# A post-norm attention and int8 layer on one core: inverse softmax divisors spread by small matmuls, y scaled on VectorE

## The reference

```python
def attention(X, Wq, Wk, Wv, Wo):            # X: (4, 1024, 512), 16 query heads, 8 key heads of 64
    q, k, v = heads(X @ Wq), heads(X @ Wk), heads(X @ Wv)
    q, k = rope(q), rope(k)                  # q*cos + rotate_half(q)*sin
    att = 50 * tanh((q @ k.T) * 256**-0.5 / 50)
    att = softmax(where(causal, att, -inf))
    return concat_heads(att @ v) @ Wo
def ffn(x):                                  # int8 per token
    scale = max(absmax(x), 1e-7) / 127
    q = clip(round(x / scale), -128, 127)
    return float16((q @ weight.T) * scale * w_scale + bias)
x = layernorm(X + attention(X, ...))
out = layernorm(x + ffn(x))
```

## Time and profile before

| | us |
|---|---|
| median of 3 runs | 1561.52 (1559.03 to 1564.63) |
| the profiled execution | 1562.01, its span 1560.3 |
| PE busy in the span | 1317.1 (84%) |
| DVE busy | 1055.1 (68%) |
| ACT busy | 843.2 (54%) |
| POOL busy | 378.6 (24%) |

### The profile page before, as it was taken

How to read it: one execution, slowest core, us unless ns; L and a number is a source line. 1 busy time by engine, 2 the same in 40 slices (tenths; PEclk the granted TensorE clock), 3 DMA queues, 4 the chain that set the end, 5 groups by cost and what they waited for, 6 DMA issues and landing times.

```text
span 1560.3 us, 17566 instructions
## 1 busy us (share of the span) xinstructions
PE 1317.1 (84%) x5776; PEld 965.0 (62%) x5776; DVE 1055.1 (68%) x1334; ACT 843.2 (54%) x952; POOL 378.6 (24%) x477
## 2 busy tenths in 40 slices
PE   6489998988687999797777999979867799999564
PEld 5366776666465777575545677756655577776442
DVE  4377887763467888683456888877346788887354
ACT  4166676652227876673223877766222577788122
POOL 2231111112542111111344111111144311121354
PEclk9789999999898999899978999999999899999797
DMA  7755445366514344447621543546562344433531
GB/s 269 255 199 139 112 128 164 79 206 188 169 54 103 104 125 112 135 95 274 176 97 54 129 109 100 130 114 190 181 198 71 97 104 107 121 87 119 183 115 48
DMA packets 124715, 212.24 MB, mean 136 GB/s; under 512 B 28112, under 2 KB 70096, under 8 KB 120400
## 3 DMA queue, kind: packets, MB, share of 16 engines
q1 hardware_dynamic: 120016, 202.72, 45.7%
q10 hardware_dynamic: 4608, 8.39, 1.4%
HBM read 105.64 MB, written 38.27 MB: 92 GB/s over the span
## 4 chain that ended last, share of the span: by engine, by line
PE 48%; SPq 13%; DVE 13%; POOL 8%; DMA 7%; issue 7%; ACT 4%; POOLq 0%; DVEq 0%; ACTq 0%
PE ps L714 18%; PE ps L633 12%; PE ps L688 12%; SPq L467 7%; POOL y_raw L1256 4%; DMA rb<-r_scratch 3%; PE ps L736 3%; SPq L480 2%; PE ps L659 2%; SPq L413 1%; DVE prob_hi L1048 1%; DVE work_r L1038 1%; PE ps L756 1%; POOL rstd L1264 1%; DMA x_raw<-X_T 1%
## 5 line engine op out<-in xcount | busy, mean ns | idle before, releaser
L714 PE MATMUL ps<-prob_hi,v 128*65 128x512 f32 (+3 forms) x1280 | 419.4, 377 | 8.3 <-DVE prob_lo L1052 8.3
L688 PE MATMUL ps<-qk 128*128 128x512 f32 (+1 forms) x1280 | 328.2, 384 | 79.1 <-ACT probs L863 38.9
L863 ACT ACTIVATE probs<-ps 128x1024 f32<-128x1024 f32 x288 | 293.2, 1018 | 169.1 <-PE ps L688 167.7
L1052 DVE TENSOR_TENSOR prob_lo<-probs,prob_hi 128x1024 fp32r<-128x1024 f32 x288 | 356.6, 1238 | 9.9
L1246 POOL TENSOR_SCALAR_AFFINE_SELECT probs<-probs 128x256 f32<-128x256 f32 (+1 forms) x192 | 146.1, 768 | 829.6 <-ACT probs L868 829.6
L688 PEld LDWEIGHTS ps<-qk 128*128 128x128 f32 x1280 | 231.4, 195 | 146.1 <-issue 38.7
L868 ACT ACTIVATE probs<-probs 128x1024 f32<-128x1024 f32 x288 | 305.6, 1061 | 8.8
L633 PE MATMUL ps<-xT,w_ring 128*128 128x512 f32 x1152 | 292.5, 399 | 16.6 <-DVE xT L992 14.7
L1048 DVE CAST prob_hi<-probs 128x1024 fp32r<-128x1024 f32 x288 | 203.3, 706 | 136.5 <-POOL probs L1246 79.7
L633 PEld LDWEIGHTS ps<-xT,w_ring 128*128 128x128 f32 x1152 | 218.7, 192 | 63.4 <-DVE xT L992 15.3
L714 PE MATMUL ps<-prob_lo,v 128*65 128x512 f32 (+1 forms) x640 | 240.8, 376 | 0.0
(11 more groups left out here) (69 smaller groups left out, 982.2 us busy)
## 6 DMA issues: line engine op xcount, KB each, us to landing
qk<-work_r SPq DMA_DIRECT2D x256, 128.0 KB, 2.3
qk<-work_r SPq DMA_DIRECT2D x512, 64.0 KB, 2.0
y_scratch<-sums SPq DMA_DIRECT2D x256, 64.0 KB
wo<-wo_scratch SPq DMA_DIRECT2D x8, 2048.0 KB, 8.8
y_raw<-y_scratch SPq DMA_DIRECT2D x32, 512.0 KB, 4.3
rb<-r_scratch SPq DMA_DIRECT2D x128, 128.0 KB, 3.3
w_ring<-w_scratch SPq DMA_DIRECT2D x15, 1024.0 KB, 5.1
x_raw<-X_T SPq DMA_DIRECT2D x16, 512.0 KB, 7.2
```

The source lines that it names most:

```text
L688: mm = nc.tensor.matmul(scores[:, g % 2, col:col + REP * w].rearrange("p (h q) -> p h q", h=REP), qk[:, n % 2, i, 2 + part, keys], qk[:, n ...
L714: mm = nc.tensor.matmul(sums_ps[:, :, GQ - w:GQ], v[:, kt, v0:v0 + width], p[:, g % ring, col:col + REP * w].rearrange("p (h q) -> p h q", ...
L863: nc.scalar.activation(probs[:, g % PRING, :], scores[:, g % 2, :], ACT.Tanh, scale=SCORE_SCALE / SOFTCAP).then_inc(capped, 1)
L1052: nc.vector.tensor_tensor(prob_lo[:, g % PRING, :], probs[:, g % PRING, :], prob_hi[:, g % HRING, :].bitcast(F32), ALU.subtract).then_inc( ...
```

## The change

The broadcast transfers go. `invert` on DVE now also splits the inverse in hi and lo (two more small instructions), `store_inverse` writes both, and `load_rows` reads for a tile four rows of 1024 values (2 heads, hi and lo) into one buffer, `rows`. `spread_rows` on PE multiplies them by a constant 4 x 128 matrix of zeros and ones in two matmuls, which puts each head's inverse on its 64 partitions in PSUM banks 2 and 3. `scale_y` moves to DVE as one instruction with that PSUM operand, and `split_y` moves to POOL. `project_v` now alternates between two PSUM banks from its third tile on. The rows are reordered on SP, PE, ACT, DVE and POOL. The low part of wo is loaded by ACT's queue, behind its last exp and ahead of its last copies of sums. In the third unit of each batch the chunks are made at steps 0, 3 and 6 where they were at 0, 5 and 9, with all that follows them, and the next X is asked for at step 9 where it was at 12, ahead of the weights.

```diff
+        def turns(u, *steps):
+
+            return tuple(s - (0, 2, 3)[x] for x, s in enumerate(steps)) if u == 2 else steps
...
-            def store_div(b, c):
-                sp.wait_ge(div_done, divs_upto(b, c))
-                sp.dma_start(r_scratch[2 * c:2 * c + 2].rearrange("t h j (a n) -> (t h j a) n", n=P // G),
-                             div[:, c, :]).then_inc(div_stored[c], 16)
-
-            def load_rb(b, i):
-                t, e = divmod(i, 2)
-                if e == 0:
-                    sp.wait_ge(div_stored[t // 2], 16 * (b + 1))
-                if i >= RBRING:
-                    sp.wait_ge(y_scaled, halves_upto(b, 0, i - RBRING))
-                for h in range(REP):
-                    sp.dma_start(rb[i % RBRING][h * HD:(h + 1) * HD, :, :].rearrange("p k n -> p (k n)"),
-                                 r_scratch[t, h, e * KO // 2:(e + 1) * KO // 2].rearrange("k n -> (k n)")
-                                 .partition_broadcast(HD)).then_inc(rb_loaded[i % RBRING], 16)
...
+            def store_inverse(b, c):
+                sp.wait_ge(inverse_lo, divs_upto(b, c))
+                for part in range(2):
+                    sp.dma_start(r_scratch[part, 2 * c:2 * c + 2].rearrange("t h j (a n) -> (t h j a) n", n=P // G),
+                                 inverse[:, part, :].bitcast(F32)).then_inc(div_stored[c], 16)
+
...
+            def load_rows(b, t):
+                sp.wait_ge(div_stored[t // 2], 32 * (b + 1))
+                if t >= 1:
+                    sp.wait_ge(rows_spread, rows_upto(b, t - 1))
+                for part in range(2):
+                    sp.dma_start(rows[REP * part:REP * (part + 1), :].bitcast(F32),
+                                 r_scratch[part, t].rearrange("h k n -> h (k n)")).then_inc(rows_loaded, 16)
...
-                        if s == 12 and m < U:
+                        if s == turns(u, 0, 0, 12)[2] and m < U:
                             sp.wait_ge(projected, chunks_upto(m, 2))
+                            if u == 2 and b + 1 < B:
+                                for part in range(XU):
+                                    load_x_turned(b + 1, part)
                             if m % UB == 0:
                                 load_wv(b + 1)
                             elif m + 1 < U:
                                 load_wq(m + 1)
-                            if u == 2 and b + 1 < B:
-                                for part in range(XU):
-                                    load_x_turned(b + 1, part)
...
+                        if u == UB - 1 and s == 14:
+                            load_div(b, 0)
                         if u == UB - 1 and s == 15:
-                            load_div(b, 0)
                             wait_put(sp, last, 1)
                             if b + 1 == B:
                                 wait_put(sp, last, 2)
                             load_y(b, 0)
                             load_y(b, 1)
-                        if u == UB - 1 and s == 17:
+                        if u == UB - 1 and s == 16:
+                            store_inverse(b, 0)
                             load_div(b, 1)
-                            store_div(b, 0)
...
                 for x in range(3):
                     wait_put(sp, last, x)
-                for i in range(RBRING):
-                    load_rb(b, i)
-                sp.wait_ge(scored, scores_upto(b, NB - 1))
-                sp.dma_start(wo[:, 1, :, :].rearrange("p k n -> p (k n)").bitcast(F32),
-                             wo_scratch[:, KO * C:2 * KO * C]).then_inc(wo_lo_loaded, 16)
+                load_rows(b, 0)
+                put_sums(b, NKV - 1, G - 2)
+                store_inverse(b, 1)
+                load_div(b, 2)
                 load_y(b, 2)
-                store_div(b, 1)
-                load_div(b, 2)
+                load_rows(b, 1)
                 put_sums(b, NKV - 1, G - 1)
-                load_rb(b, 3)
+                store_inverse(b, 2)
...
-                if t >= 6:
-                    pe.wait_ge(v_lo_done, rows_upto(b, t - 4))
+                if t >= 4:
+                    pe.wait_ge(v_lo_done, rows_upto(b, t - 2))
...
+            def spread_rows(b, t):
+                if t == 0:
+                    pe.wait_ge(spread_ready, 16)
+                    pe.wait_ge(capped, scores_upto(b, NB - 1))
+                else:
+                    pe.wait_ge(y_scaled, rows_upto(b, t - 1))
+                pe.wait_ge(rows_loaded, 32 * rows_upto(b, t))
+                for e in range(2):
+                    mm = nc.tensor.matmul(ps[:, SPREAD_BANK + e, :], spread[0:2 * REP, :],
+                                          rows[0:2 * REP, e * 512:(e + 1) * 512], start=True, stop=True)
+                mm.then_inc(rows_spread, 1)
...
                 weigh(b, NB - 1)
+                spread_rows(b, 0)
                 for t in range(NT):
                     if t <= 2 and more:
                         project_v(b + 1, 2 * t + 2)
                         project_v(b + 1, 2 * t + 3)
+                    if t + 1 < NT:
+                        spread_rows(b, t + 1)
                     if t >= 2:
                         turn_q(b, t - 2)
                     project_out(b, t, 0)
@@ -882,7 +899,7 @@
                 nc.scalar.activation(sums[0:VJ, slot, :], ps[0:VJ, PV_BANK + c % 2, :], ACT.Copy).then_inc(sums_kept, 1)
...
+                act.wait_ge(scored, scores_upto(b, NB - 1))
+                act.dma_start(wo[:, 1, :, :].rearrange("p k n -> p (k n)").bitcast(F32),
+                              wo_scratch[:, KO * C:2 * KO * C]).then_inc(wo_lo_loaded, 16)
...
                 for t in range(1, NT):
-                    if t + 1 < NT:
-                        round_y(b, t + 1)
                     if t >= 4:
                         store(b, t - 4)
                     if t >= 2:
                         keep_q(b, t - 2)
+                    if t + 1 < NT:
+                        round_y(b, t + 1)
                     norm1(b, t - 1)
...
             def invert(b, c):
                 dve.wait_ge(div_loaded[c], 16 * (b + 1))
-                nc.vector.reciprocal(div[:, c, :], div[:, c, :]).then_inc(div_done, 1)
-
-            def split_y(b, t):
-                dve.wait_ge(y_hi_done, rows_upto(b, t))
-                nc.vector.tensor_tensor(y_lo[:, y_place(t), :, :], y_raw[:, y_place(t), :, :],
-                                        y_hi[t % 2][:, :, :].bitcast(F32), ALU.subtract).then_inc(y_lo_done, 1)
+                nc.vector.reciprocal(div[:, c, :], div[:, c, :]).then_inc(inverse_done, 1)
+                dve.wait_ge(inverse_done, divs_upto(b, c))
+                if divs_upto(b, c) > 1:
+                    before = divs_upto(b, c) - 2
+                    dve.wait_ge(div_stored[before % G], 32 * (before // G + 1))
+                nc.vector.tensor_copy(inverse[:, 0, :], div[:, c, :]).then_inc(inverse_hi, 1)
+                dve.wait_ge(inverse_hi, divs_upto(b, c))
+                nc.vector.tensor_tensor(inverse[:, 1, :], div[:, c, :], inverse[:, 0, :].bitcast(F32),
+                                        ALU.subtract).then_inc(inverse_lo, 1)
+
+            def scale_y(b, t):
+                dve.wait_ge(rows_spread, rows_upto(b, t))
+                dve.wait_ge(y_loaded[t % YRING], ring_upto(b, t, YRING))
+                row = y_raw[:, y_place(t), :, :].rearrange("p k n -> p (k n)")
+                nc.vector.tensor_tensor(row, ps[:, SPREAD_BANK:SPREAD_BANK + 2, :].rearrange("p a c -> p (a c)"), row,
+                                        ALU.mult).then_inc(y_scaled, 1)
...
+                        if at := chunk_at(b, u, s, turns(u, 3, 8, 12)):
                             rope_read(*at)
-                        if u == UB - 1 and s == 17:
+                        if u == UB - 1 and s == 16:
                             invert(b, 0)
...
-                        if at := chunk_at(b, u, s, (6, 11, 15)):
+                        if at := chunk_at(b, u, s, turns(u, 6, 11, 15)):
...
                 probs_of(b, NB - 1)
                 invert(b, 1)
-                split_y(b, 0)
+                scale_y(b, 0)
                 if more:
                     split_v(b + 1, 0)
                     split_v(b + 1, 1)
-                split_y(b, 1)
+                scale_y(b, 1)
                 invert(b, 2)
                 if more:
                     split_v(b + 1, 2)
@@ -1195,16 +1228,16 @@
                     split_v(b + 1, 4)
                     split_v(b + 1, 5)
                 for t in range(1, NT):
+                    if t + 1 < NT:
+                        scale_y(b, t + 1)
                     shift_by(b, t - 1, 0, rstd1, shift1)
-                    if t + 1 < NT:
-                        split_y(b, t + 1)
-                    quantise(b, t - 1)
                     if t >= 3:
                         stats2(b, t - 3)
                     if t >= 2:
                         rescale(b, t - 2)
                     if t >= 3:
```

(20 more changed lines are left out.)

70 lines of the change are left out of this document (39 added, 31 removed).

## The result

| | before | after |
|---|---|---|
| median | 1562.78 us | 1547.8 us (1545.51 to 1549.15, 4 runs) |
| ratio | | 0.9895, 95% interval 0.9874 to 0.9916 |
| profiled execution, its span | 1562.01, 1560.3 | 1545.51, 1543.4 |

A forecast was written before the change was run, and what follows sets the result against it. The prediction took a chain through five engines, not one full engine, to bound the row phase's middle tiles. Terms 41.8 - 6.4 + 14.6 + 1.0 = 51.0 us saved gave 1510 us, range 1476 to 1546.

The forecast's parts named there:

- What bounds the kernel: Row phase's middle tiles: no engine is the bound, but a chain through five engines including scale_y and y_hi.
- the middle tiles: Four middle row-phase intervals per batch: 9.6 us a tile, bounds 8.1 and 12.1, saving 41.8 us in all.
- The hold: Middle tiles: quantise's two DVE instructions wait for POOL's split_y and first addition, 1.1 and 1.2 us late.
- Rival C: Row phase: the single buffer of rows becomes the bound, its loads waiting for spreading; slower, 1578 us; chance 0.06.
- The last interval: Row phase's last interval, without scaling: 9.5 us instead of 7.90, a loss of 6.4 us over four batches.
- The start: Start of the row phase, from last weigh to third residual1: 14.6 us gained, bounds 0 and 25.
- about 1 more since the first divisors are inverted a step earlier: Start of the row phase, first three batches: about 1 us gained per batch besides the 3.2 of PE's list.
- the 2 MB of wo's low part, now on ACT's queue: Start of the row phase: needed only at first project_out; may come late in the last batch, costing up to 5 us.
- The third unit: Third unit of each batch, closer chunks and earlier X: +1 us gained together, bounds -12 and +16.
- PE waits about 2 us: Third unit, last batch: between closer chunks DVE needs 3.7 us against 2.3 of PE work.
- lower bound of -12: Third unit: the case in which PE waits between chunks in every batch.
- X ahead of the weights: Third unit: asking for the next X before the weights gives about 1.1 us, three times.

The follow-up runs named there:

- experiment 11: experiment 10 with ACT's z (norm1) ahead of y_hi (round_y): 1526.17 us.
- experiment 12: experiment 6 with the subtraction split_y back on DVE, just ahead of quantise: 1544.9 us.
- experiment 8: Changed kernel with the row phase's loops on DVE, ACT and POOL in the old order, new scaling kept: 1546.85 us.
- experiment 10: experiment 6 with the row phase's loops on DVE, ACT and POOL in the old order: 1506.17 us.
- experiment 3: Changed kernel with the third unit's chunks back at steps 0, 5 and 9, next X at step 12 but still ahead of the weights: 1515.49 us.
- experiment 6: experiment 3 with wo's 2 MB low part asked for one instruction later on ACT, behind the first of its last two copies of sums: 1508.63 us.
- experiment 13: experiment 10 with the store of the first inverses and load of the second divisors ahead of SP's last eight chunk copies: 1520.59 us.
- experiment 4: Changed kernel with the third unit's sums stored by ACT's queue, not SP's; chunks stay close: 1543.9 us.
- experiment 1: Changed kernel with the third unit as before: chunks at steps 0, 5 and 9, next X at step 12 behind the weights: 1522.16 us.

## Why the prediction was wrong

**What bounds the kernel, and the middle tiles: right.** The chain through `scale_y` and `y_hi` was what bounded the tile. Without it PE no longer waits for `linear` (3.7 us in most tiles before, under 0.25 in the middle tiles now), and PE and DVE are the fullest engines (31.5 and 30.8 of 36.4 us). The term was 41.8 and measured 45.8. The hold was foreseen by line and by cause and over-sized: 1.5 us in a middle tile, not 2.3. Experiments 11 and 12 settle that it is a hold, since it follows whichever instruction stands beside POOL's, from 0.43 to 2.03 us in the mean for the same two lines. What the forecast did not see is that the reorder, which causes it, is worth nothing beside the new scaling (experiments 8 and 10). Rival C, the single buffer of rows as the bound, shows in one middle tile of each of the first three batches (2.1 to 2.2 us of PE), and in the last batch ahead of the middle tiles (2.3, 3.5 and 5.5 us).

**The last interval: wrong in size.** 7.9 us, as before, where 9.5 was forecast. The scaling is not held there (0.53 us), since `split_y` is missing too; the rounding is (1.28), and costs the interval nothing. The forecast carried the middle tile's delay over. The 9.5 us do occur in other kernels, as in the second and fourth batch of experiment 3, each behind a middle tile of 8.8 instead of 9.9 us, so the size depends on how the engines stand to each other when they come to it.

**The start: right behind the last `weigh`, wrong ahead of it.** 14.6 us of gain were forecast, 4.7 of loss came. The forecast counted from the last `weigh` to the third `residual1`, and there the gain came, and more: 39.6, 39.5, 39.6 and 39.2 us instead of 44.9, 43.5, 44.9 and 42.5, together 17.9 less. But the last `weigh` itself ends later behind the last tanh: 20.6, 24.4, 21.8 and 6.6 us instead of 13.8, 16.9, 13.8 and 6.3, together 22.6 more. The step that failed is the only one that looked ahead of it, "about 1 more since the first divisors are inverted a step earlier". The inversion stands ahead of the last probabilities in both kernels, so that a late divisor stops DVE and PE; DVE waits 14.3, 16.0 and 13.4 us for it where it waited 8.1, 9.2 and 7.4. The cause is the load that the text did name: "the 2 MB of wo's low part, now on ACT's queue" were costed as coming late, at up to 5 us in the last batch, where they come too early, ahead of the divisors. With the load behind the divisors the last `weigh` is 22.5 us sooner in sum, and what is left at the end is 6.9 us (experiment 6), since the second divisors and rows are then waited for. The order's part is 3.3 us in the first two intervals (experiments 6 and 10), where `quantise` is held in the second one. SP's list of the last chunk's copies is on the path too (experiment 13), but no run took them off it; how much of the start they bound stays open.

**The third unit: wrong by 28 us, outside its bounds of -12 and +16.** The failing step is "PE waits about 2 us" in the last batch. That price is right: steps 0 to 14 take 51.4 us instead of 49.0 in three batches (52.9 in the second), but it is paid four times, not once, 11 us, as the lower bound of -12 had allowed for. The rest, 32 - 11 = 21 us, was not in the working at all. It counted DVE's passes and PE's matmuls between chunks and left out what each chunk makes SP issue, 16 copies of 0.62 us, with the stores of sums behind them and ACT behind those (experiments 3 and 4). The text had named SP's list as the reason why asking earlier for X is worth little, and had not asked what stands behind the copies. X ahead of the weights was worth 6.7 us against 3.3 forecast.

## What to carry to other kernels

When work is put closer together, the busy time of the engines that compute it is half of the count. Count the issuing on the queue that serves it (here 10 us a chunk at 0.62 us a transfer), and follow who waits for what stands behind it. Look for a large load that is asked for just ahead of a small one that an engine waits for: asking for it one instruction later gave 7 us here. A forecast that counts from one event has to ask, too, whether the change moves that event. And a change of several parts should be timed by its parts; this one held 47 us of gain less 32 of loss. The parts that gain make 1515 us, and with wo's load moved 1506 to 1509.

## What the runs showed of the hardware

- In one execution (experiment 1) the same 16 KB load was used 10.2 us after its issue when 2 MB had been asked for 0.4 us earlier on another queue, and 2.6 us when it was 0.01 us ahead of them.
- DVE's rounding tensor_scalar of 128x512 took 0.43 us alone and 1.37 when started 0.37 us behind a POOL addition (1.45). The scaling one took 0.49 alone and 2.53 when started 0.12 us behind a POOL subtraction of 128x1024 (2.35). POOL's addition took 1.29 alone and 2.32 when started 0.04 us behind a DVE subtraction of two SBUF operands. The trace agrees with the Trainium skill ("SBUF — State Buffer", section "Who interferes with whom"), which says that whoever issues first has the shared ports for the whole instruction.
- DVE's product of 128x1024 with one operand in PSUM took 1.22 us in every kernel of this study, beside POOL or not.
